# State space stage of a four stage model: squares moved to ScalarE, out projection and two norms in one block, local tables loaded earlier, local copies moved ahead of the first exponentials

## What is computed

```python
y = y * jax.nn.silu(z)                                   # 256 features per token
y = y * lax.rsqrt(jnp.mean(y * y, -1, keepdims=True) + EPS) * norm_w
y = jnp.einsum('bld,ed->ble', y, out_proj_w) + x         # 256 -> 128
y = (y - mean(y)) * lax.rsqrt(var(y) + EPS) * ln_w + ln_b
x = _layernorm(x + y)                                    # a second norm, without weights
...                                                      # then, twice: shift, q, k, v; q and k scaled by
                                                         # their norms and rotated; attention in windows
```

## Time and profile before

| | us |
|---|---|
| median of 3 runs | 2046.2 (2045.5 to 2050.0) |
| the profiled execution: time, span | 2044.64, 2042.6 |
| input projection, convolution | 8.4 to 57 |
| of it: weights landed, first matmul on them; first convolution on DVE | 13.70; 18.18 |
| scan (`ssc`) | 57 to 127.3 |
| out projection (`ssd`); norms (`ssn`, `n0`) | 127.6 to 144.3; 144.7 to 158.1, 158.5 to 167.6 |
| loads (`lc`) | 167.9 to 175.2 |
| local layer 0: projection; attention | 175.5 to 246.2; to 336.2 |
| PE in `ssd`, once warm | one tile per 0.70 |
| read of an accumulator on ACT, mean | 0.196 |

### The profile page before, as it was taken

How to read it: one execution, slowest core, us unless ns; L and a number is a source line. 1 busy time by engine, 2 the same in 40 slices (tenths; PEclk the granted TensorE clock), 3 DMA queues, 4 the chain that set the end, 5 groups by cost and what they waited for, 6 DMA issues and landing times. The chain is left out here.

```text
span 2042.6 us, 36152 instructions
## 1 busy us (share of the span) xinstructions
PE 1862.5 (91%) x11446; PEld 930.9 (46%) x11446; DVE 1593.6 (78%) x2433; ACT 1270.9 (62%) x2613; POOL 1066.7 (52%) x1218
## 2 busy tenths in 40 slices
PE   5764898989868999999999999999999999999798
PEld 2552476547643444444444443444443444444446
DVE  6786866686656888887888887888888888888455
ACT  6432685368625777776777776777777677777331
POOL 0644842583215656655665664665665566566200
PEclk9997999999988999999999999999999999999799
DMA  1001122012044998998889999898998889999353
GB/s 38 1 1 69 38 46 74 6 36 47 15 156 169 343 330 322 345 327 314 321 323 333 336 329 327 301 342 323 336 337 324 313 326 329 341 326 335 128 115 73
DMA packets 201614, 454.27 MB, mean 222 GB/s; under 512 B 12065, under 2 KB 159265, under 8 KB 200257
## 3 DMA queue, kind: packets, MB, share of 16 engines
q1 hardware_dynamic: 201408, 451.76, 62.8%
HBM read 230.86 MB, written 206.83 MB: 214 GB/s over the span
## 5 line engine op out<-in xcount | busy, mean ns | idle before, releaser
L1637 ACT ACTIVATE g.probs<-g_score,g.lowest 128x1024 f32<-128x1024 f32 x514 | 568.0, 1109 | 335.4 <-DVE g.lowest L1623 331.2
L1623 DVE TENSOR_REDUCE g.lowest<-g_score 128x1 f32<-128x1024 f32 x514 | 605.5, 1219 | 185.6 <-PE g_score L1591 185.6
L1591 PE MATMUL g_score<-g.keys,g.queries 64*128 64x512 f32 x2056 | 502.3, 607 | 20.0 <-issue 11.0
L1733 DVE STREAM_TRANSPOSE g.blocks<-g.probs 128x768 f32<-128x768 f32 x512 | 467.0, 950 | 2.4 <-ACT g.probs L1637 1.5
L1653 PE MATMUL g_mix_ps<-g.far,mid.y_tok 128*64 128x512 f32 x1560 | 377.7, 605 | 0.0
L1591 PEld LDWEIGHTS g_score<-g.keys,g.queries 64*128 64x128 f32 x2056 | 183.9, 188 | 250.2 <-ACT g.probs L1637 131.5
L1693 POOL TENSOR_TENSOR g.scaled<-g.scaled,g.coef 128x1024 f32<-128x1024 f32 x66 | 125.1, 1896 | 237.9 <-ACT g.scaled L1685 230.1
L1753 POOL TENSOR_TENSOR mid.y_tok<-mid.y_tok,g.waves 128x512 f32<-128x512 f32 x128 | 162.3, 1268 | 72.8 <-ACT mid.y_tok L1606 72.8
L1613 PEld LDWEIGHTS g_turned<-top.ident,g.probs 128*128 128x128 f32 x1024 | 107.8, 141 | 195.5 <-issue 194.8
L1380 POOL TENSOR_TENSOR g.queries<-mid.y_tok 64x256 f32<-64x256 f32 x256 | 185.4, 724 | 19.6
L1613 PE MATMUL g_turned<-top.ident,g.probs 128*128 128x128 f32 x1024 | 168.8, 288 | 0.0
(11 more groups left out here) (370 smaller groups left out, 2757.4 us busy)
## 6 DMA issues: line engine op xcount, KB each, us to landing
g.far<-bounce SPq DMA_DIRECT2D x257, 768.0 KB, 7.0
bounce<-g.blocks SPq DMA_DIRECT2D x256, 768.0 KB, 6.0
e.share<-shares SPq DMA_DIRECT2D x8, 1024.0 KB, 17.8
g.far<-g.near SPq DMA_DIRECT2D x7, 768.0 KB, 12.3
lt.early<-turns SPq DMA_DIRECT2D x2, 2048.0 KB, 9.2
lt.early<-la0.v SPq DMA_DIRECT2D x6, 512.0 KB, 9.2
lt.early<-la1.v SPq DMA_DIRECT2D x6, 512.0 KB, 8.8
bounce<-g.near SPq DMA_DIRECT2D x4, 768.0 KB, 15.3
```

The lines of the kernel that those rows point to most:

```text
L1591: nc.tensor.matmul(score[:, 2 * pair + odd], queries[rows, turn, head, cols], keys[rows, turn, head, pair * CH:(pair + 1) * CH], start=Tru ...
L1623: nc.vector.tensor_reduce(lowest[:, unit, half, r:r + 1], score[:, 2 * half:2 * half + 2].rearrange("p b n -> p (b n)"), AX.X, ALU.max, ne ...
L1637: nc.scalar.activation(probs[:, r % 2, half * 2 * CH:(half + 1) * 2 * CH], score[:, 2 * half:2 * half + 2].rearrange("p b n -> p (b n)"), ...
L1733: ins = nc.vector.transpose(blocks[:, r, :, REST * half:REST * (half + 1)].rearrange("p j t c -> p t j c"), probs[:, r % 2, at:at + REST * ...
```

## The change

1. In the scan ACT squares `gate[:, c - 2]` at the end of its chunk c and sums along the row (`square_sum`); behind the loop it runs a Sqrt on one column, which loads that table, and the square of tile 14.
2. `ssd`, `ssn` and `n0` become one block, `output_and_norms`. Every engine works in groups of four tiles. ACT applies both norms' scale and offset (Identity with both operands per partition), the second one for two of four tiles, DVE for the other two. `ln_b` is added to x by POOL in the input projection (into `out_tok`).
3. The tables of the local transformer get their memory ahead of the state space; SP loads them in the scan's block. `moved` and the band's cast go into the new block, the block `lc` is gone. SP clears the retired semaphores in layer 0.
4. In both local layers ACT runs a one column exponential (which loads the table) and `take_pairs(14)` ahead of `exps(0)`.

```diff
 def state_space(nc, dram, const, tables, x_tok, out_tok):
...
                 def _(pool):
                     nc.gpsimd.memset(raw[:, :, 0:TAPS - 1], 0.0).then_inc(pads, 1)
+                    nc.gpsimd.memset(eps[:], EPS).then_inc(eps_ready, 1)
+                    pool.wait_ge(const["x_loaded"], 16)
+                    pool.wait_ge(w_loaded, 7 * 16)
+                    nc.gpsimd.tensor_tensor(out_tok[:], x_tok[:], ln_b.unsqueeze(1).broadcast_to([P, T, D]), ALU.add)\
+                        .then_inc(biased, 1)
...
+                def _(sync):
+                    load_tables(sync, dram, tables)
+                    def squares(c):
+                        act.wait_ge(m["gated"], c + 1)
+                        nc.scalar.activation(squared[:, c % 2], gate[:, c], ACT.Square, accum_out=square_sum[:, c:c + 1])
                         if c >= 1:
                             scale_state(c - 1)
+                        if c >= 2:
+                            squares(c - 2)
+                    act.wait_ge(eps_ready, 1)
+                    nc.scalar.activation(warm[:], eps[:], ACT.Sqrt)
+                    squares(T - 2)
-        with Space(nc, "ssd") as sd:
...
-        normalise(nc, "ssn", out_tok, out_tok, ln_w, ln_b, x_tok)
-    normalise(nc, "n0", out_tok, out_tok)
+        output_and_norms(nc, const, tables, gate, square_sum, eps, w_out, ln_w, x_tok, out_tok)
+def output_and_norms(nc, const, tables, gate, square_sum, eps, w_out, ln_w, x_tok, out_tok):
...
+            def _(act):
+                def take(t):
+                    act.wait_ge(m["turn_done"], t + 1)
+                    if t >= 2:
+                        act.wait_ge(m["prod_done"], t - 1)
+                    nc.scalar.activation(yT[:, t % 2], turned[:, t % 2, 0:INNER], ACT.Copy).then_inc(m["yT_ready"], 1)
+                def root(which, g):
+                    act.wait_ge(var[which], g + 1)
+                    nc.scalar.activation(spread[:, which, group(g)], moments[:, which, group(g), 1], ACT.Sqrt,
+                                         bias=eps[:, 0:1]).then_inc(std[which], 1)
+                def normed(which, g, rows, done, count=4):
+                    act.wait_ge(offset_ready[which], g + 1)
+                    for t in range(4 * g, 4 * g + count):
+                        ins = nc.scalar.activation(rows[:, t], rows[:, t], ACT.Identity,
+                                                   bias=offset[:, which, t:t + 1], scale=spread[:, which, t:t + 1])
+                    ins.then_inc(done, 1)
+                take(0)
+                nc.scalar.activation(squared[:], gate[:, T - 1], ACT.Square, accum_out=square_sum[:, T - 1:T])\
+                    .then_inc(m["total_ready"], 1)
+                act.wait_ge(m["total_ready"], 1)
+                nc.scalar.activation(rms[:], square_sum[:], ACT.Sqrt, bias=eps[:, 0:1], scale=1.0 / INNER)\
+                    .then_inc(m["rms_ready"], 1)
+                for t in range(1, 6):
+                    take(t)
+                for g in range(NC):
+                    root(0, g)
+                    take_from, take_to = 6 + 4 * g, min(T, 10 + 4 * g)
+                    for t in range(take_from, min(take_from + 2, take_to)):
+                        take(t)
+                    if g >= 1:
+                        root(1, g - 1)
+                    normed(0, g, h, m["centred"])
+                    for t in range(take_from + 2, take_to):
+                        take(t)
+                    if g >= 1:
+                        normed(1, g - 1, out_tok, m["normed"], 2)
+                root(1, NC - 1)
+                normed(1, NC - 1, out_tok, m["normed"], 2)
+            def _(dve):
...
+                for g in range(NC + 1):
+                    if g < NC:
+                        sums(g)
+                    if g >= 2:
+                        scales(1, g - 2)
+                        normed_too(g - 2)
+                    if g >= 1:
+                        weigh(g - 1)
+                    if g < NC:
+                        moments_of(0, g, h, m["summed"], 1)
+                    if g >= 1:
+                        moments_of(1, g - 1, out_tok, m["added"], 0)
+                    if g < NC:
+                        scales(0, g)
+                scales(1, NC - 1)
+                normed_too(NC - 1)
...
 def project_and_attend(nc, dram, const, tables, layer, src, dst, wo, qkT, v, inverse):
...
                 sync.dma_start(wo[:], dram[f"wo{layer}"]).then_inc(m["wo_loaded"], 16)
-                if layer:
-                    clear_retired(sync)
+                clear_retired(sync)
...
                 take_pairs(T - 3)
+                nc.scalar.activation(warm[:], const["ones"][:, 0:1], ACT.Exp)
+                take_pairs(T - 2)
                 exps(0)
-                take_pairs(T - 2)
                 take_pairs(T - 1)
```

262 lines of the change are left out of this document (115 added, 147 removed).

## The result

The changed kernel takes 2018.12 us (median of 4 runs, 2017.2 to 2019.02) beside 2046.38 for the kernel before. The ratio is 0.9859 with a 95% interval of 0.9842 to 0.9876, so it is faster by 28 us, 25 to 32.

A forecast was written before the change was run, and what follows sets the result against it. The 48 us up to layer 0 were taken as serial DVE work plus exposed loads, the scan as DVE-bound. -16.9 - 1.3 - 1.9 - 1.7 = -21.8 us gave 2024.4 us, range 2019.5 to 2033.

The forecast's parts named there:

- Squares in the scan: Scan loop: ACT's 14 squares, one per chunk, two chunks behind, fit its idle time; cost 0.
- Loads and small moves: Loads moved into the scan remove the gap block, about 7.5 us; semaphore clears cost 0, bias add 0, at worst 0.5.
- The new block: Scan's end to layer 0: queue-by-queue walk in groups of four tiles puts layer 0's start at 158.6 for 175.50, -16.9 us.
- A: New block: hand-offs between ACT and DVE and upper prices make it end at 163.9, +5.7 us, 2030.1; chance 0.11.
- E: New block: groups do not overlap, 15.0 us each, 60 for four; +9 us, 2055; chance 0.02.
- Rival B: New block: PE loses its clock, all matmuls at half clock, walk ends at 162.4; +4.1 us, 2028.5; chance 0.10.
- The hole in layer 0: Layer 0's projection: DVE's 1.27 us hole before tile 4, from GpSimd's late first keys, closes; -1.3 us.
- Copies ahead of the exponentials: Both local layers: tile 14's copies before exps(0) bring exps(1) earlier, -1.9 us in layer 0, -1.7 in layer 1.
- a stall of 0.9 in the v moves' time that may go: Possible extra gain of 0.9 us, counted only in the lower end of the range.
- Rival C: Attention's start is held by something else, so earlier exps(1) gain nothing; +3.6 us, 2028.0; chance 0.10.
- The rule on table loads: Skill page: a table switch takes about 2.66 us; by it tile 14's copies come 1.3 later per layer, sum 2.6 smaller.
- the lower walk: New block with all lower-end prices together: the walk ends at 157.1, counted as -1.1 us in the range.

The follow-up runs named there:

- loads_back: The changed kernel with the local transformer's loads and the band's cast put back into a block of their own behind the new one: 2026.71 us.
- after_again: The changed kernel run and profiled once more, unaltered, for the spread of its stages: 2018.18 us.

## Why the prediction was right, and where it was wrong

**Squares in the scan: right.** Forecast cost 0, "finished at about 89.9, with 1.1 us to spare"; 1.27 are left, and doubled squares still leave 0.86.

**Loads and small moves: right within 1 us.** 7.5 for the gap; loads_back gives 6.6 to 7.3 by the stages and 8.6 by medians. The bias addition costs nothing where it is, and 0.7 to 0.9 at the start of the new block.

**The new block: the mechanism right, the size 1.0 too small.** Forecast 31.3 from the scan's end to layer 0, measured 29.7 to 30.9. From the end of DVE's first four sums to layer 0 the walk had 25.4 and the traces have 25.0, in all four profiles: 0.4 of it. The rest is "PE's products of tiles 0 to 3 come at the half clock", which I took from the one profile as a constant: the first sums end 5.9 and 5.6 us behind the scan in the two profiles with the low clock, where the walk had 5.9, and 4.6 in the two at full clock. Even in the profile before, only three of the four products were slow; the row that the walk ends on, 0.61 at 132.24, is at full clock. Rivals A (163.9) and E (60 us for the block) didn't occur. Rival B didn't either: from 134 to 147 the granted clock was 1.00 in the first profile and in after_again.

**The hole in layer 0: right in size (-1.4 for -1.3), incomplete in cause.** I put it to GpSimd's late first keys alone. Kernels with late angles and no hole show that the low clock behind PE's wait was needed for it. Part of the match is luck: the clock could have stayed up before.

**Copies ahead of the exponentials: layer 0 right by luck (-1.8 for -1.9), layer 1 half of what came (-3.4 for -1.7).** The step that failed is the last sentence there, "The next exponentials follow exps(1) directly in both", by which the walk took the move of exps(1) for the whole gain. In layer 1 exps(1) moved by 1.9 for 1.7, but a wait of 1.7 for POOL's probabilities lay 9 us further on and went as well, in the first profile of before with a projection at half clock behind it. The trace that I had before me shows it, 1.73 at 468.45; I had reckoned with the like in layer 0 only, and named it there "a stall of 0.9 in the v moves' time that may go".

In layer 0 two errors met. The walk has PE turn tile 15 at full clock, in about 1.1 us; it took 1.94 in all four profiles, and exps(1) come 5.56 or 6.28 us behind the table load instead of 5.34. Against that, with tile 14 turned at full clock the attention still became 2.8 us shorter, and with the low clock 0.9. The mean of the four is -1.8, and no single profile shows it. Rival C, which would have eaten the gain, is refuted in both layers.

**The rule on table loads.** The Trainium skill ("ScalarE: Activation LUTs", What ACT_TABLE_LOAD costs) would have the exponential 2.66 us behind the load. In the rows above the one column exponential starts 1.30 us behind it (229.74, 231.04), and the copies 0.11 later. The measurement decides; the 2.6 us that the rule would have taken off my sum were not lost.

**The total.** 24.6 of the 26.8 us lie in the four stages of the table, 2.8 more than the sum: 1.0 in the block, 1.7 in layer 1. The remaining 2.2 would have to lie in the rest, whose differences of 12 us in seven profiles allow it; nothing shows that the change shortened anything there, and the cause of this part stays open. The first result of 28.3 was a favourable draw of another 1.5.

**The range** was too narrow at the bottom. I had given 2 to 3 us to differences between runs and 1.1 to the lower walk. The changed kernel's single times have a standard deviation of 3.0, and what one profile shows of the low clock went into the sum as if it stood there always. Two of the first (5.9), the lower walk (1.1), the clock at the block's start (1.2) and the stall of 0.9 below 2024.4 would have asked for 2015.3; that is worked out afterwards.

## What to carry to other kernels

Before costing a part, see whether the slow rows in it are at the low clock: they can be part of the draw and not of the code, and a second profile of the same kernel is the cheapest experiment there is. When two versions are compared row by row, compare profiles that have the same clock at that place. When a step is moved earlier, follow the chain to the next point where an engine had no slack, not to the first instruction that gains. And a table load belongs into a wait that the engine has anyway: behind the copies instead of ahead of them, it put off the first exponentials by 1.4 us.

## What the runs showed of the hardware

- A DVE cast of 128x512 to bf16 took 4.96 us beside a GpSimd addition of 4.52, and 0.48 without it: tenfold, and it ended 0.5 us behind GpSimd's instruction.
- The granted clock at one and the same place differs between executions of one kernel: the block's first product took 0.71 or 1.20, PE's turn of tile 14 in layer 0 1.07 or 1.94 (with it attention 0 86.5 or 88.5). The first convolution started at 18.4 to 20.1 in the changed kernel, which fits the clock without being shown to be it.
- TensorE's low clock at a stage's start can be bought off with matmuls that nobody reads (granted clock 1.00 instead of 0.50, 1.8 us less in projection 0, four times of four), which the total did not show.
